# Six edge passes written without hardware loops, and 192 tiles' attention scalars gathered by GpSimd beside a shortened lookup loop

## The chip, the core and the metric

The kernel runs on one core of a Trainium2 chip. TensorE (PE) does matrix products into PSUM, VectorE (DVE) and ScalarE (ACT) do elementwise work, GpSimd (POOL) issues the indirect DMAs here, and SyncE (SP) issues the others. Each engine has its own instruction stream; they meet at semaphores. The metric is the device time of one execution in microseconds, the median over runs of the same kernel; lower is better. The profile is of one execution.

## What is computed

A graph with 6250 nodes of 128 features and 106,250 directed edges sorted by destination goes through four blocks, each followed by `x = layernorm(x + block(x))`:

```python
edge_index = jnp.stack([src, dst])
x = _layernorm(x + _L0_gnn_ref(...))   # mean of neighbours' rows, then a linear layer
x = _layernorm(x + _L1_gnn_ref(...))   # SAGE, SAGE, GAT (2 heads), RGCN (4 relations), fusion
x = _layernorm(x + _L2_gnn_ref(...))   # edge MLP with batch norm, summed by source
x = _layernorm(x + _L3_gnn_ref(...))   # 8 relations, edge weights
```

Every block contains a sum over edges, `segment_sum(table[src] * weight, dst)`. The attention layer also needs one pair of scalars for each edge, looked up by its source:

```python
al_src = (h * a_src).sum(-1)
al_dst = (h * a_dst).sum(-1)
e = jax.nn.leaky_relu(al_src[src] + al_dst[dst], 0.2)
```

## The kernel before

The edges lie in 832 tiles of 128 (T = 832, U = 16, ITERS = 52). `aggregate` sums over edges and is called six times, in this order: block0, sage1, sage2, gat, rgcn and block3. For each tile POOL gathers 128 rows of the table by an indirect DMA into one of U = 16 message buffers (line 387). DVE builds a one-hot matrix of the edges' positions in a window of 128 nodes (`one_hot`, lines 399 and 402; two for gat's two heads), PE multiplies the message by it into one of HU = 8 PSUM windows (line 534), and DVE adds the window into the accumulator at a node offset that depends on the data (line 458). DVE reads eight such offsets at a time into registers (`bases`, line 295), twice in 16 tiles. Four conditions tie the engines together: POOL reuses a message buffer when PE's product of 16 tiles earlier is done (`tile_done`); PE waits for the one-hot (`hot_ready`), for the gather to land (`gathered`) and, every second tile, for a window that DVE has added (`window_used`); DVE waits for `tile_done`.

POOL's stream in `aggregate` is already written out, one instruction a gather. PE, DVE, ACT (sage1's edge sort) and SP (gat's own rows) run hardware loops (`Fori`), whose body is one turn of 16 tiles; in block0's second part and in sage1 it is three and four turns. In a loop the semaphore values and the columns of the tables follow the loop's variable, so that register instructions stand before the waits and the operands. Line 487 is DVE's and line 552 PE's loop in gat and rgcn, 492 DVE's in block3. Five more jobs ride along in the turns: block0 counts and ranks the edges by source, sage1 sorts records, gat adds each node's own term, rgcn adds a part of the fusion (line 419), and block0 adds a bias.

`attention_terms` comes between sage2 and the softmax. POOL first writes 49 scatters of `al` to `t_last` (line 1414) and waits for them. Beside it the other engines look the source's two scalars up for all 832 tiles, four tiles (a quad) at a time: SP loads the keys (line 1408), PE spreads them over the partitions (line 1507), ACT makes a one-hot of them (lines 1368 and 1370), PE looks up with 12 matmuls (line 1498), DVE multiplies by a second one-hot and reduces (lines 1472, 1481, 1463), and ACT stores the result in `m.e` (line 1424). The first iteration of eight quads is written out, the other 25 are a loop. The next stage starts behind a barrier.

Of the kernel before, what the change touches and what calls it, by code (L numbers as in the profile page):

```python
# [26 lines left out]
P = 128  # L27
# [4 lines left out]
NT = -(-NODES // P)  # L32
# [3 lines left out]
ROWS = NT * P  # L36
# [3 lines left out]
QU = 4  # L40
QUADS = U // QU
ITERS = -(-EDGES // (P * U))
T = ITERS * U
EB = -(-T // P)
TP = EB * P
# [10 lines left out]
G = 13  # L56
# [260 lines left out]
def aggregate(nc, m, phase, table, index, weights, blocks, clear=True, degree=False, clears_tables=False, slots=False, sorts=None, own=False, fuses=None, loads=(), chunks=None, bias=None):  # L317
# [9 lines left out]
    n = e.passes  # L327
# [3 lines left out]
    with ExitStack() as ctx:  # L331
        sb, pb, sem = place(nc, ctx, phase)
# [25 lines left out]
        if own:  # L358
            @block.sync
            def _(sp):  # L360
                with sp.Fori(0, NT, 1) as it:
                    sp.wait_ge(own_made, it)
                    sp.dma_start(own_rows[:], table[bass.ds(it * P, P), :]).then_inc(own_in, 16)

# [5 lines left out]
        if sorts:  # L370
            @block.sync
            def _(sp):
                sort.load(sp)

            @block.scalar
            def _(act):
                with act.Fori(0, G, 1) as n:
                    for q in range(GT // QU):
                        sort.spread_low(act, n, q)

# [14 lines left out]
        def _(dve):  # L395
# [75 lines left out]
                    sort.keep(dve, of_sort[0])  # L471

            if slots:
                with dve.Fori(0, G, 1) as it:
                    turn(it, False, counts=it)
                order.find_starts(dve)
                dve.wait_ge(weights_in, 16 * len(loads))
                for first, last, added in ((0, NG, bias), (NG, G, None)):
                    with dve.Fori(first, last, 1) as n:
                        for r in range(TURNS - 1):  # L480
                            turn(n * (TURNS - 1) + (G + r), False, ranks=(n, r), bias=added if r == 0 else None)
            elif sorts:
                with dve.Fori(0, G, 1) as n:
                    for r in range(TURNS):
                        turn(n * TURNS + r, False, of_sort=(n, r))
            elif own or fuses:
                with dve.Fori(0, NT, 1) as it:
                    turn(it, True)
                with dve.Fori(NT, ITERS, 1) as it:
                    turn(it, False)  # L490
            else:
                with dve.Fori(0, ITERS, 1) as it:
                    turn(it, False)

        @block.tensor
        def _(pe):
            def own_terms(it):
                pe.wait_ge(own_in, 16 * (it + 1))
                pe.wait_ge(own_hot_ready, heads * (it + 1))
                pe.wait_ge(own_used, it)  # L500
                for b in range(blocks):
                    for j in range(heads):
                        f = (j * blocks + b) * P
                        last = nc.tensor.matmul(ps_own[:, b, :], own_rows[:, f:f + P], own_hot[:, j * P:(j + 1) * P],
                                                start=(j == 0), stop=(j == heads - 1))
                last.then_inc(own_made, 1)

            def fuse(it):
                pe.wait_ge(own_used, it)
                for k in range(2):  # L510
                    last = nc.tensor.matmul(ps_own[:, 0, :], fuses.weight[:, k, :], fuses.nodes[:, k, bass.ds(it * P, P)], start=(k == 0), stop=(k == 1))
                last.then_inc(own_made, 1)

            def turn(it, nodes_too, counts=None, ranks=None, of_sort=None):
                for u in range(U):
                    k = u % HU
                    if u % 2 == 0:
                        pe.wait_ge(e.window_used, used0 + it * U + u + 2 - HU)
                    if counts is not None and u % 2 == 1:
                        order.add_up(pe, counts, u // 2)  # L520
                    if ranks is not None:
                        order.rank_up(pe, ranks[0], ranks[1] * U + u)
                    if of_sort is not None:
                        sort.move(pe, of_sort[0], of_sort[1] * U + u)
                    if nodes_too and own and u == HU:
                        own_terms(it)
                    if nodes_too and fuses and u == HU:
                        fuse(it)
                    pe.wait_ge(e.hot_ready, hots0 + (it * U + u + 1) * heads)
                    pe.wait_ge(e.gathered[u], 16 * (turns0 + it + 1))  # L530
                    for b in range(blocks):
                        for j in range(heads):
                            f = (j * blocks + b) * P
                            last = nc.tensor.matmul(ps[k][:, b, :], message[u][:, f:f + P], hot[:, u, j * P:(j + 1) * P],  # L534
                                                    start=(j == 0), stop=(j == heads - 1))
                    if degree:
                        last = nc.tensor.matmul(ps[k][:, 1, :], m.ones[:], hot[:, u, :], start=True, stop=True)

                    last.then_inc(e.tile_done, 1)

            if slots:
                with pe.Fori(0, G, 1) as it:
                    turn(it, False, counts=it)
                with pe.Fori(0, G, 1) as n:
                    for r in range(TURNS - 1):
                        turn(n * (TURNS - 1) + (G + r), False, ranks=(n, r))
            elif sorts:
                with pe.Fori(0, G, 1) as n:
                    for r in range(TURNS):
                        turn(n * TURNS + r, False, of_sort=(n, r))  # L550
            elif own or fuses:
                with pe.Fori(0, NT, 1) as it:
                    turn(it, True)
                with pe.Fori(NT, ITERS, 1) as it:
                    turn(it, False)
            else:
                with pe.Fori(0, ITERS, 1) as it:
                    turn(it, False)


# [812 lines left out]
def attention_terms(nc, m, a):  # L1373
# [3 lines left out]


    AQ = 8
    AITERS = T // (AQ * QU)  # L1380
    assert T % (AQ * QU) == 0
    with ExitStack() as ctx:
        sb, pb, sem = place(nc, ctx, "al")
        table, rest, part = m.al, sb("rest", [P, 2, NT]), sb("part", [P, 2, NT])
# [2 lines left out]
        low_hot, distance = sb("low_hot", [P, 2, QU * P], BF16), sb("distance", [P, 2, QU * P])  # L1387
        high_hot, product = sb("high_hot", [P, 2, QU, NT]), sb("product", [P, 2, QU, 2, NT])
        picked = sb("picked", [P, 2, QU, 2])
        ps_low = [pb(f"ps_low{k}", [P, QU * P]) for k in range(2)]  # L1390
        ps = [pb(f"ps{k}", [P, QU, P]) for k in range(2)]
        keys_in, spread, low_ready, looked, high_ready, product_ready, reduced, kept = (
# [5 lines left out]

        @block.sync
        def _(sp):  # L1400
            sp.wait_ge(ints_padded, 2)
            for k, name in enumerate(("dst", "edge_type_4")):
                load_edges(sp, m.edge_ints[:, k], a[name], 1, ints_in)
            sp.wait_ge(ints_in, 96)
            with sp.Fori(0, AITERS, 1) as it:
                for q in range(AQ):
                    sp.wait_ge(spread[q], it)
                    sp.dma_start(keys[:, q], row_of(m.t_low_dst[bass.ds(((it * AQ + q) * QU) * P, QU * P)])).then_inc(keys_in[q], 16)

        @block.gpsimd  # L1410
        def _(pool):
            for j in range(NT):
                rows = P if j < NT - 1 else TAIL
                pool.indirect_dma_start(m.t_last, bass.IndirectOffsetOnAxis(ap=m.last_edge[0:rows, j:j + 1], axis=0), table[0:rows, j, :],
                                        None).then_inc(placed, 16)
            pool.wait_ge(placed, 16 * NT)

        @block.scalar
        def _(act):
            def keep(it, q):  # L1420
                act.wait_ge(zeroed, 1)
                act.wait_ge(reduced[q], it + 1)
                tiles = bass.ds((it * AQ + q) * QU, QU)
                nc.scalar.copy(m.e[:, :, tiles].rearrange("p k t -> p t k"), picked[:, q % 2]).then_inc(kept[q], 1)
# [15 lines left out]
                look(it, False)  # L1440
            for q in range(AQ - 2, AQ):
                keep(AITERS - 1, q)

        @block.vector
        def _(dve):
# [1323 lines left out]
def gnn_blocks(nc, a):  # L2769
    with ExitStack() as ctx:  # L2770
        sb, _, sem = place(nc, ctx, "all")
        m = Memory()
# [3 lines left out]
        table = lambda name, *shape: nc.dram_tensor(name, shape, F32, kind="Internal").ap()  # L2776
# [3 lines left out]
        m.t_hidden, m.t_self = table("t_hidden", C, T2 * P), table("t_self", TP * P, 2)  # L2780
        m.t_chunks, m.t_rec_dst = table("t_chunks", TABLE + G * P * CHUNKS, CHUNK * REC), table("t_rec_dst", P, TP * REC)
        m.t_rec = m.t_chunks[0:TABLE, :].rearrange("c (r k) -> (c r) k", k=REC)
        m.t_last = table("t_last", TP * P, 4)
        m.t_attr = nc.dram_tensor("t_attr", (ATTR, TP * P), BF16, kind="Internal").ap()
        m.t_w1c = nc.dram_tensor("t_w1c", (ATTR, C), BF16, kind="Internal").ap()
        m.t_low_dst, m.t_low = (nc.dram_tensor(n, (TP * P,), BF16, kind="Internal").ap() for n in ("t_low_dst", "t_low"))
# [98 lines left out]
```

## Time and profile before

| | |
|---|---|
| time, median of 3 runs | 10762.2 us (10758.03 to 10766.74) |
| the profiled execution's own time | 10761.99 us |
| its span, first to last instruction | 10760.2 us |
| instructions in the span | 143680 |
| busy share: PE, DVE, ACT, POOL | 57%, 47%, 14%, 59% |
| mean granted TensorE clock | 0.707 |
| HBM read and written | 794.65 MB, 144.18 MB |

An engine's busy time counts instructions that its datapath runs; register, branch and semaphore instructions belong to its sequencer and aren't in it. "Idle before" is the time in which an engine had no instruction before the ones of the row, with what ended most of it; "issue" means that the profile shows nothing that was waited for, and "remote" a semaphore event without a named instruction. Where a row says x832, 832 instructions are in the group. A table by window gives for each stretch its length and, for each engine, busy time and number of instructions.

### The profile page before, as it was taken

Reading aid. Unit: us, or ns where it says so; the run is one execution under the profiler, and the core shown is the slowest. Engines: PE = TensorE matmul, PEld = TensorE weight load, DVE = VectorE, ACT = ScalarE, POOL = GpSimd, SP = SyncE. Lnnn points to the kernel's source line nnn. Section 1 sums busy time; section 2 is a strip of 40 time slices with the busy share of each in tenths; the row PEclk is TensorE's granted clock in tenths of the full one; section 3 lists DMA queues with packets and bytes.
Section 4 is the critical chain, followed back from the end, with each engine's and each line's share of the span. In section 5 each row is a group of like instructions: output and inputs, shape, how many; then the busy total and the mean of one; then the engine's idle time right before and its main releaser. Section 6 shows DMA issues by size and latency. Waiting matters only on the chain. (4 is left out here: it accounts for less than half of the span.)

```text
span 10760.2 us, 143680 instructions
## 1 busy us (share of the span) xinstructions
PE 6118.1 (57%) x32219; PEld 5125.3 (48%) x32219; DVE 5059.5 (47%) x17185; ACT 1560.0 (14%) x3639; POOL 6324.8 (59%) x6901
## 2 busy tenths in 40 slices
PE   4555566665555546755777753444555567853333
PEld 4445455554555533535777633333444456733332
DVE  6666755554444421685666633334211115733334
ACT  0000033332000001740000000000221225710000
POOL 6666466775666662106666546664566666646665
PEclk7777778887666668558999965555666768965555
DMA  2111211112333312005666521112655656421111
GB/s 78 43 45 45 59 47 45 45 45 61 90 91 90 91 55 73 4 11 145 185 185 185 165 79 46 46 46 57 147 156 155 159 155 145 151 92 46 46 46 47
DMA packets 651433, 941.53 MB, mean 88 GB/s; under 512 B 253820, under 2 KB 427892, under 8 KB 650812
## 3 DMA queue, kind: packets, MB, share of 16 engines
q0 software_dynamic: 252288, 606.77, 21.1%
q1 hardware_dynamic: 299360, 328.15, 9.9%
q10 hardware_dynamic: 99548, 4.42, 0.8%
q14 instruction: 207, 1.70, 0.1%
q8 instruction: 30, 0.49, 0.0%
HBM read 794.65 MB, written 144.18 MB: 87 GB/s over the span
## 5 line engine op out<-in xcount | busy, mean ns | idle before, releaser
L534 PE MATMUL block_windows<-block_hot,block_message 128*128 128x128 f32 x3328 | 871.1, 393 | 881.3 <-DVE third_acc L458 418.1
L534 PE MATMUL sage_windows<-sage_hot,sage_message 128*128 128x128 f32 x4992 | 959.3, 357 | 584.2 <-DVE sage_hot L402 396.2
L534 PEld LDWEIGHTS sage_windows<-sage_hot,sage_message 128*128 128x128 f32 x4992 | 925.1, 267 | 679.3 <-DVE sage_hot L402 452.7
L534 PEld LDWEIGHTS block_windows<-block_hot,block_message 128*128 128x128 f32 x3328 | 741.0, 286 | 979.9 <-issue 624.2
L2214 POOL DMA_INDIRECT eh_message<-t_q,all_position x896 | 848.5, 947 | 533.3 <-issue 248.0
L387 POOL DMA_INDIRECT block_message<-t_rel,all_src x832 | 789.8, 949 | 576.2 <-issue 209.3
L387 POOL DMA_INDIRECT sage_message<-t_x,all_src x832 | 870.4, 1046 | 425.4 <-issue 217.2
L387 POOL DMA_INDIRECT rgcn_message<-t_rel,all_src x832 | 788.7, 948 | 520.9 <-issue 204.4
L458 DVE TENSOR_TENSOR first_acc<-first_acc,sage_windows 128x128 f32 (+1 forms) x1664 | 588.2, 353 | 1063.9 <-remote 596.6
L387 POOL DMA_INDIRECT block_message<-in_x,all_src x832 | 818.8, 984 | 434.7 <-issue 204.0
L534 PE MATMUL gat_windows<-gat_hot,gat_message 128*128 128x128 f32 x6656 | 901.9, 293 | 287.9 <-issue 207.6
L387 POOL DMA_INDIRECT gat_message<-t_h,all_src x832 | 790.0, 949 | 461.9 <-remote 202.9
L387 POOL DMA_INDIRECT sage_message<-t_s,all_src x832 | 789.5, 949 | 458.6 <-issue 197.7
L534 PEld LDWEIGHTS gat_windows<-gat_hot,gat_message 128*128 128x128 f32 x6656 | 852.7, 208 | 333.7 <-issue 331.6
L838 PE MATMUL sage_ps_sort<-first_acc,sage_sort_low_hot 128*128 128x272 f32 x1664 | 601.1, 495 | 444.6 <-DVE first_acc L803 183.5
L2244 DVE TENSOR_SCALAR_CACHE_REDUCE eh_hot<-eh_low_rows,all_column 128x128 f32<-128x128 bf16 x896 | 248.2, 343 | 1100.6 <-DMA eh_low_rows<-t_low 805.1
L534 PE MATMUL rgcn_windows<-rgcn_hot,rgcn_message 128*128 128x128 f32 x1664 | 441.5, 437 | 559.0 <-DVE second_acc_rgcn L458 311.0
L2271 PE MATMUL eh_ps<-eh_hot,eh_window 128*128 128x128 f32 x1792 | 517.9, 385 | 379.6 <-issue 246.7
L534 PEld LDWEIGHTS rgcn_windows<-rgcn_hot,rgcn_message 128*128 128x128 f32 x1664 | 376.5, 319 | 619.9 <-issue 425.3
L2271 PEld LDWEIGHTS eh_ps<-eh_hot,eh_window 128*128 128x128 f32 x1792 | 407.2, 280 | 463.8 <-issue 335.3
L838 PEld LDWEIGHTS sage_ps_sort<-first_acc,sage_sort_low_hot 128*128 128x128 f32 x1664 | 361.2, 241 | 528.0 <-issue 412.9
L458 DVE TENSOR_TENSOR second_acc<-second_acc,gat_windows 128x256 f32 x832 | 347.9, 418 | 406.9 <-remote 247.5
(474 smaller groups left out, 11739.8 us busy)
## 6 DMA issues: line engine op xcount, KB each, us to landing
eh_window<-t_p SPq DMA_DIRECT2D x896, 64.0 KB
t_hidden<-eh_hidden SPq DMA_DIRECT2D x112, 512.0 KB
sc_rows<-t_hidden SPq DMA_DIRECT2D x112, 512.0 KB
eh_low_rows<-t_low SPq DMA_DIRECT2D x112, 256.0 KB
t_rel<-n_h SPq DMA_DIRECT2D x49, 512.0 KB, 2.6
eh_message<-t_q,all_position POOLq DMA_INDIRECT x896
block_message<-in_x,all_src POOLq DMA_INDIRECT x832
sage_message<-t_x,all_src POOLq DMA_INDIRECT x832
```

What stands on the lines that cost most here:

```text
L387: pool.indirect_dma_start(message[u][:], None, table, bass.IndirectOffsetOnAxis(ap=index[:, it * U + u:it * U + u + 1], axis=0)).then_inc( ...
L458: nc.vector.tensor_tensor(window, window, ps[k], ALU.add).then_inc(e.window_used, 1)
L534: last = nc.tensor.matmul(ps[k][:, b, :], message[u][:, f:f + P], hot[:, u, j * P:(j + 1) * P], start=(j == 0), stop=(j == heads - 1))
L838: last = self.nc.tensor.matmul(self.ps[:, 0:SPAN * REC], self.low_hot[:, k, t], self.masked[:, k, t].rearrange("p h k -> p (h k)"), start= ...
L2214: pool.indirect_dma_start(message[:, u, :], None, m.t_q, bass.IndirectOffsetOnAxis(ap=m.dst[:, it * U + u:it * U + u + 1], axis=0)).then_i ...
L2244: nc.vector.tensor_scalar(hot[:, q, e], rows, m.column[:], 0.0, ALU.is_equal, ALU.add, accum_out=m.of_source[:, bass.ds(it * U + q * QU + ...
L2271: nc.tensor.matmul(ps[q][:, e], window[:, u, :], hot[:, q, e], start=False, stop=False, skip_group_check=True)
```

## The change

Every `Fori` in `aggregate` becomes a Python loop, so that all 52 turns of each pass are written out, with constants for the semaphore values and table columns. What the turns do and wait for stays; the node offsets are still read into registers. In `attention_terms` the lookup loop covers 20 iterations (640 tiles) in place of 26. SP writes `al` to a new table in memory, `t_al`. POOL, after its 49 scatters, waits for that table and gathers the pairs of the last 192 tiles from it, one indirect DMA a tile, into `rows_got`, with a wait in front of each batch of 16 for the batch two before it. At the end ACT waits for all of them and copies them into `m.e`.

```diff
-                with sp.Fori(0, NT, 1) as it:
+                for it in range(0, NT):
                     sp.wait_ge(own_made, it)
...
-                with act.Fori(0, G, 1) as n:
+                for n in range(0, G):
                     for q in range(GT // QU):
                         sort.spread_low(act, n, q)
...
             elif sorts:
-                with dve.Fori(0, G, 1) as n:
+                for n in range(0, G):
                     for r in range(TURNS):
                         turn(n * TURNS + r, False, of_sort=(n, r))
             elif own or fuses:
-                with dve.Fori(0, NT, 1) as it:
+                for it in range(0, NT):
                     turn(it, True)
-                with dve.Fori(NT, ITERS, 1) as it:
+                for it in range(NT, ITERS):
                     turn(it, False)
             else:
-                with dve.Fori(0, ITERS, 1) as it:
+                for it in range(0, ITERS):
                     turn(it, False)
...
-    AITERS = T // (AQ * QU)
-    assert T % (AQ * QU) == 0
+    AITERS = 20
+    LOOKED = AITERS * AQ * QU
+    GOT = T - LOOKED
+    assert 0 < GOT and GOT % 16 == 0
...
+        rows_got = sb("rows_got", [P, GOT, 4])
+        got = [sem(f"got{k}") for k in range(2)]
+        table_kept = sem("table_kept")
...
+            sp.dma_start(m.t_al.rearrange("(j p) w -> p j w", p=P), table[:]).then_inc(table_kept, 16)
             sp.wait_ge(ints_padded, 2)
...
+            pool.wait_ge(table_kept, 16)
+            for n in range(GOT):
+                batch, turn = divmod(n, 16)
+                if batch >= 2 and turn == 0:
+                    pool.wait_ge(got[batch % 2], 16 * 16 * (batch // 2))
+                pool.indirect_dma_start(rows_got[:, n, :], None, m.t_al,
+                                        bass.IndirectOffsetOnAxis(ap=m.src[:, LOOKED + n:LOOKED + n + 1], axis=0)).then_inc(got[batch % 2], 16)
             pool.wait_ge(placed, 16 * NT)
...
+            for k in range(2):
+                act.wait_ge(got[k], 16 * sum(1 for n in range(GOT) if n // 16 % 2 == k))
+            nc.scalar.copy(m.e[:, :, LOOKED:T].rearrange("p k t -> p t k"), rows_got[:, :, 0:2])
```

The same replacement stands in PE's three branches and in DVE's branch for block0, not shown.

## Rows read from the trace of the kernel before

**Rows 1.** Page: busy time by engine, and its slices of POOL, TensorE clock and DMA.

```profile
PE 6118.1 (57%) x32219; PEld 5125.3 (48%) x32219; DVE 5059.5 (47%) x17185; ACT 1560.0 (14%) x3639; POOL 6324.8 (59%) x6901
...
POOL 6666466775666662106666546664566666646665
PEclk7777778887666668558999965555666768965555
DMA  2111211112333312005666521112655656421111
```

**Rows 2.** Windows of the six passes and the lookup loop: length, then busy time (x instructions).

```profile
core 0: us, PE busy (x) PEld busy (x) DVE busy (x) ACT busy (x) POOL busy (x), PEclk, DMA share, GB/s
50.00:650.00 600.00, 321.59 (x1799) 294.42 (x1799) 386.44 (x1112) 0.00 (x0) 398.27 (x402) 0.73 0.18 47
1350.00:2540.00 1190.00, 765.52 (x3251) 631.94 (x3252) 683.78 (x2040) 400.79 (x1010) 843.50 (x808) 0.80 0.17 45
2700.00:3870.00 1170.00, 636.80 (x3226) 597.12 (x3227) 480.83 (x1615) 0.00 (x0) 764.95 (x807) 0.68 0.31 90
4910.00:6140.00 1230.00, 951.80 (x6912) 888.54 (x6913) 782.79 (x2594) 0.00 (x0) 778.63 (x821) 0.93 0.65 185
6270.00:7450.00 1180.00, 480.25 (x1826) 407.05 (x1827) 436.17 (x1674) 0.00 (x0) 777.71 (x822) 0.53 0.18 46
9510.00:10690.00 1180.00, 436.12 (x1639) 365.36 (x1638) 423.02 (x1625) 0.00 (x0) 781.50 (x825) 0.54 0.18 46
```

**Rows 3.** Timeline of rgcn from 7020.5 us: start, duration, instruction, [idle before].

```profile
7020.53 0.95 POOL L387 DMA_INDIRECT rgcn_message<-t_rel,all_src  x1 [0.30 <-issue]
7023.60 0.95 POOL L387 DMA_INDIRECT rgcn_message<-t_rel,all_src  x1 [2.12 <-remote]
```

**Rows 4.** Timeline of gat from 5510.8 us.

```profile
5510.87 0.27 PE L534 MATMUL gat_windows<-gat_hot,gat_message 128*128 128x128 f32 x1 [0.25 <-issue]
...
5511.60 0.36 PE L534 MATMUL gat_windows<-gat_hot,gat_message 128*128 128x128 f32 x1 [0.46 <-issue]
5512.31 0.27 PE L534 MATMUL gat_windows<-gat_hot,gat_message 128*128 128x128 f32 x1 [0.35 <-issue]
...
5513.02 4.28 PE L534 MATMUL gat_windows<-gat_hot,gat_message 128*128 128x128 f32 x36 [0.44 <-issue]
```

**Rows 5.** Timeline of the lookup's first 70 us, DVE's products, SP's keys, POOL's last scatter.

```profile
4309.55 67.61 SPq L1408 DMA_DIRECT2D al_keys<-t_low_dst  x18
...
4316.21 0.57 DVE L1481 TENSOR_TENSOR al_product<-al_ps,al_high_hot 128x392 f32<-128x392 f32 x1 [9.94 <-DMA neigh_neigh_bias<-in_L_gnn_b_neigh]
...
4337.23 0.57 DVE L1481 TENSOR_TENSOR al_product<-al_ps,al_high_hot 128x392 f32<-128x392 f32 x1 [19.72 <-remote]
...
4361.60 1.57 POOL L1414 DMA_INDIRECT t_last<-all_al,all_last_edge  x1 [0.30 <-issue]
4368.02 0.57 DVE L1481 TENSOR_TENSOR al_product<-al_ps,al_high_hot 128x392 f32<-128x392 f32 x1 [29.47 <-issue]
```

**Rows 6.** Windows: 45.7 us beside POOL's scatters, and 313 us without POOL.

```profile
4316.30:4362.00 45.70, 3.39 (x26) 2.09 (x26) 2.52 (x6) 3.00 (x6) 34.72 (x37) 0.50 0.03 2
4380.50:4693.50 313.00, 313.00 (x2505) 201.36 (x2502) 251.62 (x577) 289.16 (x578) 0.00 (x0) 0.50 0.00 1
```

**Rows 7.** Groups of 4380.5 to 4693.5 us, and POOL's small gathers of the softmax.

```profile
L1370 ACT ACTIVATE al_low_hot<-al_distance,all_ones 128x512 bf16<-128x512 f32 x193 | 139.3, 722 | 6.4
...
L1652 POOL DMA_INDIRECT softmax_rows<-t_self,all_last_edge x49 | 46.4, 947 | 487.3 <-SPq L1621 472.7 <-issue 14.6
```

**Rows 8.** Timeline at the end of the lookup: ACT's last store.

```profile
4702.88 0.20 ACT L1424 COPY attention_e<-al_picked 128x8 f32<-128x8 f32 x1 [1.26 <-DVE al_picked L1463]
```

**Rows 9.** DMA queues that load instructions: sage1 (first two rows), sage2 (last).

```profile
q14 instruction: 81, 0.66, 0.2%
q8 instruction: 2, 0.03, 0.0%
...
q14 instruction: 7, 0.06, 0.0%
```

More of the change, by code:

```diff
@@ L473, in _ @@
             if slots:
-                with dve.Fori(0, G, 1) as it:
+                for it in range(0, G):
                     turn(it, False, counts=it)
@@ L478, in _ @@
                 for first, last, added in ((0, NG, bias), (NG, G, None)):
-                    with dve.Fori(first, last, 1) as n:
+                    for n in range(first, last):
                         for r in range(TURNS - 1):
@@ L541, in _ @@
             if slots:
-                with pe.Fori(0, G, 1) as it:
+                for it in range(0, G):
                     turn(it, False, counts=it)
-                with pe.Fori(0, G, 1) as n:
+                for n in range(0, G):
                     for r in range(TURNS - 1):
@@ L547, in _ @@
             elif sorts:
-                with pe.Fori(0, G, 1) as n:
+                for n in range(0, G):
                     for r in range(TURNS):
@@ L551, in _ @@
             elif own or fuses:
-                with pe.Fori(0, NT, 1) as it:
+                for it in range(0, NT):
                     turn(it, True)
-                with pe.Fori(NT, ITERS, 1) as it:
+                for it in range(NT, ITERS):
                     turn(it, False)
             else:
-                with pe.Fori(0, ITERS, 1) as it:
+                for it in range(0, ITERS):
                     turn(it, False)
@@ L2782, in gnn_blocks @@
         m.t_rec = m.t_chunks[0:TABLE, :].rearrange("c (r k) -> (c r) k", k=REC)
-        m.t_last = table("t_last", TP * P, 4)
+        m.t_last, m.t_al = table("t_last", TP * P, 4), table("t_al", ROWS, 4)
         m.t_attr = nc.dram_tensor("t_attr", (ATTR, TP * P), BF16, kind="Internal").ap()
```

## The prediction, made before the changed kernel was built or run

> **What bounds the kernel now.** I read the page's busy shares and its 40 slices first, then the windows of the six passes, then single instructions inside them. No engine is full: POOL has the most, 59%, and in the passes' slices it stands at 6 or 7 tenths with DMA mostly at 1 or 2 [rows 1]. In the windows of the passes POOL works two thirds of the time, PE between 37% and 77%, DVE 34 to 64% [rows 2]. So the passes are bounded by a handover, not by a datapath.
>
> A gather occupies POOL 0.95 us and the next follows after 0.30 us of issue [rows 3]: 1.25 us each, 20.0 us for a turn of 16 tiles. The passes need more. From the gathers in each window [rows 2], 16 of them take 600/402 x 16 = 23.9 us in block0, 1190/808 x 16 = 23.6 in sage1, 23.2 in sage2, 24.0 in gat, 23.0 in rgcn and 22.9 in block3. What stands above 20.0 is POOL waiting for `tile_done`, as the 2.12 us in [rows 3]. Over 52 turns and six passes: (3.9 + 3.6 + 3.2 + 4.0 + 3.0 + 2.9) x 52 = about 1070 us, of which POOL waits some 955 (sage1's gathers are themselves a little longer, 843.50/808 = 1.04 us, and a few of the window's POOL instructions aren't gathers). 955 us is the ceiling of what the first part can bring.
>
> Why does POOL wait, when PE and DVE have time to spare? In gat PE starts one matmul each 0.7 us (5510.87, 5511.60, 5512.31), each only 0.27 to 0.36 us long, and then, in the stop of POOL, 36 of them back to back in 4.28 us [rows 4]. The same picture stands in the lookup. While POOL scatters, the quads of `attention_terms` come 21.0 and 30.8 us apart (4316.21, 4337.23, 4368.02); POOL's last scatter starts at 4361.60 and ends at 4363.17, and 4.9 us later the quads run [rows 5]. Then they take 313.0/(578/3) = 1.624 us each, with ACT busy 289 of 313 us (a quad is three instructions of ACT, x193 for each line) [rows 6, 7]. In 45.7 us beside the scatters PE did 26 matmuls where it does 366 without them [rows 6]. I read this as: while POOL issues indirect DMAs back to back, every other engine's stream advances in steps of 0.7 us, and catches up when POOL stops.
>
> **Part 1, the passes.** Removed are, per tile and estimated from the code, some 1.5 register or branch instructions of PE's stream and 2.5 of DVE's; 832 x 6 tiles make 7,500 and 12,500. All wait conditions, gathers, matmuls and DVE operations stay, and so does `bases`. None of it shortens POOL's 20.0 us for a turn; what can shrink is the stop. SP's and ACT's loops (gat's rows, sage1's sort) are off this path: ACT has 400 us of work in sage1's 1190, and gat's own rows are one load a turn.
>
> What a removed instruction is worth I take from passes that differ in work per tile. Matmuls and weight loads for a tile: gat 2 x 6912/821 = 16.84, sage2 2 x 3226/807 = 8.0, block3 2 x 1639/825 = 3.97 [rows 2]. From sage2 to gat a turn grows by 0.77 us, 0.087 for each instruction a tile; from block3 to sage2 by 0.32 us, 0.079. So the engines' work weighs little: twice as much makes the stop only a quarter longer. By 0.083 us a turn, PE's 1.5 give 0.083 x 1.5 x 52 x 6 = 39 us, PE's and DVE's 4 together 104 us if both lay on the path in turn. I take 70. The bounds are 0 (the steps belong to waits and datapath instructions, all of which stay) and 150 (a register instruction costs more than a matmul's step).
>
> The price of straight code is its supply. Sage1, whose turns stand four times in the loop's body, loads 83 packets of instructions and sage2 7 [rows 9], and the two differ by 0.36 us a turn, 19 us over the pass; at most 19/76 = 0.25 us a packet, all put down to them. Seven packets for sage2's written-out 807 gathers are some 115 instructions each. The six passes hold about 52,400 instructions of PE and DVE, estimated from the windows' counts and the code's waits, so some 456 packets: below 115 us, and near 0 if they are loaded ahead. I count nothing, since sage1's queue was busy 0.66 us in all [rows 9], and keep the bound as a rival.
>
> **Part 2, the lookup.** Now its loop ends with ACT's store at 4702.88 [rows 8]. Removed: six iterations, 48 quads x 1.624 = 78 us. Added on SP: one store of `al`, ahead of the loads of integers and keys in its queue; it is out some tens of us before POOL's 49 scatters end, and hides behind them. Added on POOL: 192 gathers. The nearest row is the softmax's small gathers, 947 ns with 14.6/48 = 0.30 us of issue [rows 7], so 192 x 1.25 = 239 us, with the waits on `got` met long before (the batch was issued 20 us earlier). POOL starts them where its scatters end, 4363.2, and ends at 4602.6. In terms of POOL this fits beside 112 quads with room to spare. But it puts POOL back into the state in which a quad takes 21 to 31 us [rows 5].
>
> Step by step: from 4316.2, the first quad's product, to 4602.6 are 286.4 us, in which 286.4/30.8 = 9.3 to 286.4/21.0 = 13.6 quads follow it; 10.3 to 14.6 of 160 are done. POOL stops, recovery takes 4.9 us as at 4368.02, and 145.4 to 149.7 quads follow at 1.624: 236 to 243 us. The loop ends at 4607.4 + 240 = 4847, to 4851 at most, 4844 at least. ACT's copy of 192 x 2 values adds 0.5 to 1 us (a store of 8 takes 0.20 [rows 8]), and the next stage stands behind a barrier, so all of it reaches the end. 4848.5 - 4702.9 = **+146 us**. The quads beside gathers may also go faster than beside scatters (0.95 against 1.57 us [rows 3, 5]). Gathers leave no more room between issues, 0.30 us in both [rows 3, 5], and gat's matmul each 0.7 us stood beside gathers. By those 0.7 us a quad, which has 13 matmuls and as many loads, would take about 26 x 0.7 = 18 us: 15.7 quads in 286 us, no different. The bounds are the two below: no slowing (-78) and no progress at all, 4607.4 + 159 x 1.624 = 4866, +164.
>
> **Sum.** The profiled execution: 10762.0, its span 10760.2 and 1.8 around it; the median is 10762.2. 10762 + 146 - 70 = **10838 us**. With part 1 between 0 and 150: 10908 to 10758.
>
> **Rivals.** *Loops are what holds the engines in the passes* (faster). If a large part of the 0.7 us steps are branches and register instructions, or what follows a branch, the stops shrink far more than by the slope. A third of them, 318 us: 10762 + 146 - 318 = 10590. For it: each turn of the loops ends in a branch, and gat's single matmuls are shorter than their spacing [rows 4], so something else fills the time. Against: the 0.7 us steps stand inside a turn as well, and sage1, with one branch in four turns, is not faster than sage2 with one in each [rows 2]. It decides from a gain above 150 us. The Trainium skill, "Runtime: NRT & Kernel Launch", section on instruction fetch, says that a taken branch breaks the sequential prefetch and that kernels prefer full unrolling where possible; by that rule straight code is the faster one, and this rival is what it would make here. The packets show only that loops load less [rows 9].
>
> *The lookup runs at full speed beside the gathers* (faster). Then its loop goes on from 4368.0 with 158 quads: 4624.6, 78 us earlier, and 10762 - 78 - 70 = 10614. It needs the 21 and 31 us to come from something else than POOL, as SP's keys, 18 loads spread over 67.61 us [rows 5]. Against: the release comes within 5 us of POOL's last scatter, and 26 matmuls in 45.7 us [rows 6] isn't a matter of keys alone. Between this and the forecast lies a loop that is slowed partly; it breaks even on part 2 where 48 quads fit into the gathers' 239 us.
>
> *Straight code isn't supplied in time* (slower still). If each packet stalls its engine by 0.23 us in a pass, that is 456 x 0.23 = 105 us where the forecast has none, and nothing is gained: 10762 + 146 + 105 = 11013. The point is a stall that isn't caught up in POOL's burst, since POOL runs 4 to 16 gathers ahead. Against: POOL's own written-out stream shows 0.30 us between gathers throughout [rows 3].
>
> **How the numbers follow.** Forecast 0.55, loops 0.23, full speed 0.12, supply 0.10. About 0.2%, 21 us, is what a measurement of this kernel can tell from no change. Of the forecast's 0.55, 0.07 lie within 21 us of the time before (part 1 at 125 to 150) or next to it; the two faster rivals have 0.35, of which 0.01 falls short. Faster 0.34, same 0.08, slower 0.58. The range reaches from below the first two rivals, 10560, to above the forecast's own upper end, 10930; outside stay the supply rival and the deep end of the first. The forecast's own range is 10758 to 10908.
>
> **What the profile after would show.** Part 2: 192 gathers of POOL 1.25 us apart from 4363 to 4603, `al_product` every 21 to 31 us until then, the stage ending about 4848; at 4625 the third case holds, and any rate above one quad in 5 us makes the part a gain. Part 1: paces lower by 0.2 us a turn in all six passes, POOL's stops still some 3 us long a turn; stops of 2 us or less mean the first rival. The instruction queues show some 450 packets more; a pass slower than before means they cost. I would be wrong above all if POOL's gathers from a small table leave the others more room than its scatters do, or if what moves in 0.7 us steps is the register instructions themselves.

## The result, and the profile after

The changed kernel takes 10859.9 us (median of 4 runs, 10850.7 to 10862.7) where the kernel before takes 10763.7: a ratio of 1.0088, with a 95% interval of 1.0071 to 1.0106. That is 96 us slower. The forecast was 10838. The profiled execution has a span of 10848.9 us, 88.7 more than before.

First the page of the changed kernel: busy time, and the two queues that load instructions.

```profile
PE 5979.3 (55%) x31595; PEld 4980.0 (46%) x31595; DVE 5020.3 (46%) x17041; ACT 1494.9 (14%) x3496; POOL 6519.6 (60%) x7093
...
q8 instruction: 205, 3.36, 0.1%
q14 instruction: 281, 2.30, 0.1%
```

No engine has changed its share by more than two points [rows 1]; POOL has 192 instructions more. The six passes, each in a window of its own (length, then busy time and instructions by engine, as in [rows 2]):

```profile
core 0: us, PE busy (x) PEld busy (x) DVE busy (x) ACT busy (x) POOL busy (x), PEclk, DMA share, GB/s
50.00:650.00 600.00, 318.68 (x1823) 290.55 (x1822) 390.47 (x1130) 0.00 (x0) 409.14 (x409) 0.72 0.18 48
1330.00:2500.00 1170.00, 710.54 (x3232) 589.67 (x3232) 689.41 (x2023) 399.75 (x1004) 840.15 (x806) 0.81 0.17 46
2650.00:3810.00 1160.00, 629.30 (x3237) 582.48 (x3235) 504.87 (x1606) 0.00 (x0) 764.07 (x806) 0.68 0.32 92
5040.00:6240.00 1200.00, 951.60 (x6825) 892.12 (x6826) 770.73 (x2565) 0.00 (x0) 779.07 (x811) 0.91 0.66 189
6390.00:7550.00 1160.00, 464.51 (x1818) 376.69 (x1819) 429.62 (x1665) 0.00 (x0) 770.83 (x813) 0.57 0.18 46
9620.00:10770.00 1150.00, 454.55 (x1603) 353.14 (x1603) 414.79 (x1593) 0.00 (x0) 764.30 (x808) 0.54 0.18 46
```

Length by gathers times 16 gives 23.5, 23.2, 23.0, 23.7, 22.8 and 22.8 us a turn, against 23.9, 23.6, 23.2, 24.0, 23.0 and 22.9 before [rows 2]. From the start of its first to that of its last gather each pass is 14.2, 16.6, 10.6, 15.2, 10.7 and 9.7 us shorter, **77 us** in sum.

The lookup goes the other way. DVE's products beside POOL's gathers, POOL's last gather, TensorE's next matmuls, and the end of the stage:

```profile
4528.93 0.57 DVE L1497 TENSOR_TENSOR al_product<-al_ps,al_high_hot 128x392 f32<-128x392 f32 x1 [35.09 <-issue]
...
4560.66 1.09 POOL L1427 DMA_INDIRECT al_rows_got<-t_al,all_src  x1 [0.30 <-issue]
4565.33 0.57 DVE L1497 TENSOR_TENSOR al_product<-al_ps,al_high_hot 128x392 f32<-128x392 f32 x1 [35.09 <-issue]
...
4570.97 1.16 PE L1514 MATMUL al_ps<-al_parts,al_low_hot 128*128 128x98 bf16 x12 [34.70 <-ACT al_low_hot L1370]
...
4589.14 0.57 DVE L1497 TENSOR_TENSOR al_product<-al_ps,al_high_hot 128x392 f32<-128x392 f32 x1 [22.50 <-issue]
...
4833.87 0.20 ACT L1437 COPY attention_e<-al_picked 128x8 f32<-128x8 f32 x1 [1.26 <-DVE al_picked L1479]
4833.98 0.85 ACT L1458 COPY attention_e<-al_rows_got 128x384 f32<-128x384 f32 x1
```

A quad comes each 36.4 us (4528.93, 4565.33), seven times in a row. The ninth product starts 3.6 us after the last gather's end (4561.75), the tenth at 4589.14, and then the loop runs at 1.63 us a quad. From POOL's first scatter to the softmax's first copy the stage takes 583.5 us against 404.3: **+179 us**. 179 less 77 are 102; the 88.7 of the spans come with another 13.5 us that stages with unchanged code are shorter by (the edge MLP 6.5 of them).

### The profile page after: what moved, and what is told of

It reads as the page before. It is cut to its first block and busy times, and to the rows that moved or that the text cites. A ratio compares the mean times of both kernels' runs of the same rounds, so it can differ in the third digit from the quotient of the medians.

```text
span 10848.9 us, 122823 instructions
## 1 busy us (share of the span) xinstructions
PE 5979.3 (55%) x31595; PEld 4980.0 (46%) x31595; DVE 5020.3 (46%) x17041; ACT 1494.9 (14%) x3496; POOL 6519.6 (60%) x7093
## 5 line engine op out<-in xcount | busy, mean ns | idle before, releaser
L534 PE MATMUL block_windows<-block_hot,block_message 128*128 128x128 f32 x3328 | 893.5, 391 | 832.5 <-DVE third_acc L458 416.5
L534 PE MATMUL sage_windows<-sage_hot,sage_message 128*128 128x128 f32 x4992 | 935.0, 349 | 586.2 <-DVE first_acc L458 356.3
L534 PEld LDWEIGHTS sage_windows<-sage_hot,sage_message 128*128 128x128 f32 x4992 | 888.9, 258 | 684.3 <-DVE first_acc L458 388.5
L534 PE MATMUL gat_windows<-gat_hot,gat_message 128*128 128x128 f32 x6656 | 939.3, 297 | 317.9 <-issue 224.6
L534 PEld LDWEIGHTS gat_windows<-gat_hot,gat_message 128*128 128x128 f32 x6656 | 876.1, 210 | 376.5 <-issue 363.3
L838 PE MATMUL sage_ps_sort<-first_acc,sage_sort_low_hot 128*128 128x272 f32 x1664 | 563.8, 470 | 472.5 <-DVE first_acc L803 308.0
L534 PEld LDWEIGHTS rgcn_windows<-rgcn_hot,rgcn_message 128*128 128x128 f32 x1664 | 349.7, 292 | 714.3 <-DVE second_acc_rgcn L458 352.6
L458 DVE TENSOR_TENSOR third_acc<-third_acc,block_windows 128x128 f32 x832 | 239.4, 288 | 713.5 <-remote 447.8
```

The costliest lines, as they stand in the source:

```text
L458: nc.vector.tensor_tensor(window, window, ps[k], ALU.add).then_inc(e.window_used, 1)
L838: last = self.nc.tensor.matmul(self.ps[:, 0:SPAN * REC], self.low_hot[:, k, t], self.masked[:, k, t].rearrange("p h k -> p (h k)"), start= ...
```

## The experiments

The chips fall into two kinds. The traces of before and after show stops and slow quads. The experiments ran on chip 11, where the kernel before takes 10865 us and every trace shows the same stops, and on chips 5 and 4, where it takes 9339 and 9355 us and the traces show none to speak of. I call the first kind held and the second free. Each kernel was timed against the kernel before on its own chip. Of the kernel before and of the changed one there are traces from the first measurement alone, whose chip isn't on record. It was held but not like chip 11: with the same code the six passes take 7206 us in the changed kernel's trace and 7284 us in that of e1b on chip 11, a difference as large as what the passes gain. So e1b's gain is read from its timing beside the kernel before, not from the traces. Chip 11 was held at two times, chips 5 and 4 were free at one time each; whether it is the chip, or something else that was there at the time, no run separates.

From POOL's first scatter to the softmax's first copy, all kernels:

| kernel | held chips | free chip 5 |
|---|---|---|
| before, or passes alone (e1, e1b) | 404.3, 404.6 us | 353.5 us |
| the change, or its lookup alone (e2) | 583.5 us | 315.5 us |
| gathers after the loop (e3, e3b) | 581.7 us | 536.3 us |
| 1.2 gathers a quad (e4, e4b) | 411.7 us | 314.8 us |
| a third of the lookup's matmuls (e5) | 532.7 us | |
| memsets for gathers (e6) | 326.4 us | |

**Each part alone (chip 5, free).** e1 has the changed `aggregate` and the old lookup, e2 the old `aggregate` and the changed lookup.

> Part 1 alone: the six passes written out, the lookup as before. In the trace of the changed kernel the six passes' gathers (first to last) are 77 us shorter in sum (14.3, 16.5, 10.6, 15.2, 10.7, 9.8) and the other stages some 14 us. If the two parts don't touch each other: 10764 - 77 to 91 = 10673 to 10687. If part of what the passes gained comes from the changed lookup or its place in the code, less: above 10700.

> Part 2 alone: loops kept, 192 gathers beside a lookup loop of 20 iterations. The changed kernel's lookup, from POOL's first scatter to the last store, took 582 us where it took 402.7: +179. So 10764 + 179 = 10943, if the parts add up. If instead the written-out passes make the lookup slower (its loop's instructions stand behind far more code), less than +160.

Measured: e1 9343.8 against 9339.2, ratio 1.0005 (0.9996 to 1.0014); e2 9298.9, ratio 0.9954 (0.9939 to 0.9969). Neither expectation holds: they were worked out for a held chip, and this one is free. Windows of e1: gat and rgcn.

```profile
4270.00:5280.00 1010.00, 880.80 (x6900) 810.84 (x6899) 780.78 (x2591) 0.00 (x0) 764.78 (x806) 1.00 0.76 223
5420.00:6420.00 1000.00, 632.09 (x1794) 436.86 (x1794) 469.58 (x1652) 0.00 (x0) 756.03 (x801) 0.50 0.20 53
```

Here 16 gathers take 1010/806 x 16 = 20.0 us, POOL's floor of [rows 3], with 0.95 us busy and 0.30 of issue. POOL never stops, so there is nothing that written-out code could shorten, and no cost of its supply shows either. And e2 beside its gathers, 220 us:

```profile
3776.00:3996.00 220.00, 219.56 (x1763) 141.42 (x1761) 177.13 (x407) 202.52 (x405) 165.72 (x174) 0.50 0.06 2
```

405 ACT instructions, three a quad, are 135 quads in 220 us: 1.63 us each beside 174 gathers. On this chip the change does what it says.

**The passes alone (chip 11, held).** The kernel of e1 again.

> The same kernel as e1_passes_only, six passes written out and the lookup as before, wanted on a chip with the slowdown. There the kernel after 49 scatters and memsets took 10705 beside 10877 before, of which the lookup explains 78 (48 quads), so some 94 are left for the passes. Theory, written-out code shortens the stops of POOL: 75 to 95 us less than before, ratio 0.991 to 0.993. Rival, the 94 are the difference between single executions: ratio 0.997 to 1.003. On a chip without the slowdown: 1.0005 again.

Measured: 10783.3 against 10865.0, ratio 0.9929 (0.9911 to 0.9946), 82 us less, as expected. It agrees with the 77 us of the two traces, and separates the part from the lookup.

**Gathers after the loop.**

```diff
             pool.wait_ge(table_kept, 16)
+            pool.wait_ge(kept[AQ - 1], AITERS)
```

> The changed kernel with POOL's 192 gathers held back until the last quad is stored, so nothing runs beside them. Theory: beside back-to-back gathers the others as good as stand still (36.4 us a quad in place of 1.62), so overlapping them is worth nothing: the loop ends at 4253 + 63 + 5 + 158 x 1.624 = 4577, the gathers add 192 x 1.25 to 1.28 = 240 to 246, end 4818 to 4825 against 4834 with overlap; 10845 to 10852, a little faster than the changed kernel. Rival, the overlap hides a useful part and the loss lies elsewhere (a table write, the end of the stage): more than 10900.

> The same kernel as e3_after_loop, wanted on a chip with the slowdown: gathers only after the last quad. 26 TensorE instructions a quad at 1.40 us each beside gathers (36.4 with 26, 14.0 with 10) mean that some 7 quads, 11 us, run beside the 240 us, and their release came 28 us after the last gather's start; so serial is 0 to 20 us faster than the changed kernel, the stage from the first scatter to the last store 560 to 582 us against 582. Rival, overlap is worth something on this chip: over 600. On a chip without the slowdown 9528 again.

Measured: on chip 5 9528.3, ratio 1.0197 (1.0181 to 1.0213), so there the overlap is worth 221 us of the stage (536.3 against e2's 315.5). On chip 11 one execution took 10969.9 (before: 10865.0), 105 us more, where the changed kernel took 96 more in the first measurement. Its stage takes 581.7 us, against 583.5 with overlap in the changed kernel: the overlap is worth nothing there. The last quad and POOL's first and last gather in e3b:

```profile
4625.35 0.20 ACT L1438 COPY attention_e<-al_picked 128x8 f32<-128x8 f32 x1 [1.26 <-DVE al_picked L1480]
4626.34 0.99 POOL L1428 DMA_INDIRECT al_rows_got<-t_al,all_src  x1 [262.09 <-ACT attention_e L1438]
...
4866.78 0.95 POOL L1428 DMA_INDIRECT al_rows_got<-t_al,all_src  x1 [0.30 <-issue]
```

**One gather at a time.**

```diff
             for n in range(GOT):
+                quad = n * (LOOKED // QU) // GOT
+                pool.wait_ge(kept[quad % AQ], quad // AQ + 1)
```

> The changed kernel with POOL waiting, before gather n, for the quad 160 n / 192 to be stored: 1.2 gathers a quad, spread over the loop. Theory a, a gather takes its 1.25 us from everybody wherever it stands: 158 x 1.624 + 240 us as in the serial kernel, 10845 to 10870. Theory b, what stops the others is that POOL has the next gather queued behind each: with pauses a gather's 0.95 us hide beside a quad and the stage ends near 4577 + 10 to 40 us: 10605 to 10640. Theory c, a single gather delays a quad by more than its own length: the stage gets longer than with all of them back to back, above 10900.

> The same kernel as e4_one_a_quad, wanted on a chip with the slowdown: each gather waits for its quad, 1.2 gathers a quad. If only an unbroken row of gathers holds TensorE, and each pause of POOL lets it catch up, a quad takes 1.63 to 3 us and the stage from the first scatter to the last store 320 to 550 us. If TensorE gets one instruction for each 1.40 us whenever a gather is under way and runs freely otherwise, a quad takes 1.63 + 1.2 x 1.25 = 3.1 us, 560 us in all, as serial. If a single gather costs more than its length, over 600.

> The kernel of e4 once more, timed on a chip with the slowdown, as the candidate that beats both: passes written out, 1.2 gathers for each quad. Its single execution there was 10795 where the kernel before took 10865: ratio 0.992 to 0.995 against before; with the lookup taking 412 us against 583 in the changed kernel, some 170 us under that one. On a chip without the slowdown 0.995, as e4.

Measured on chip 11: one execution of 10794.9 (before: 10865.0), the stage 411.7 us. Theory a (560 us) and theory c fall. Theory b has the right sign but not the size: by its 4577 + 10 to 40 the stage would have been 334 to 364 us. A window of e4b, 327 us beside its gathers:

```profile
4375.00:4702.00 327.00, 257.12 (x2026) 162.95 (x2026) 201.22 (x467) 234.70 (x467) 177.96 (x187) 0.50 0.05 2
```

Two of its gathers in the timeline, with what they waited for:

```profile
4387.94 0.94 POOL L1429 DMA_INDIRECT al_rows_got<-t_al,all_src  x1 [2.84 <-ACT attention_e L1439]
...
4391.20 0.94 POOL L1429 DMA_INDIRECT al_rows_got<-t_al,all_src  x1 [0.89 <-ACT attention_e L1439]
```

467 ACT instructions are 156 quads in 327 us: 2.10 us each with 187 gathers among them, where 36.4 us stood beside an unbroken row in the changed kernel. On the free chips the pauses cost nothing: 0.9952 (0.9937 to 0.9967) on chip 5, as e2 without them, and 0.9967 (0.9953 to 0.9981) on chip 4. e4c ran on chip 4 too, so on a held chip this kernel has one execution and no interval.

**Fewer TensorE instructions (chip 11).** The kernel computes with one of the table's three bf16 parts, so its attention terms are less exact.

```diff
-                    for n in range(3):
+                    for n in range(1):
...
-parts[:, n].rearrange("p k j -> p (k j)"), start=(n == 0), stop=(n == 2))
+parts[:, n].rearrange("p k j -> p (k j)"), start=(n == 0), stop=(n == 0))
```

> The changed kernel with 4 matmuls for a quad's lookup in place of 12 (only the first of the three bf16 parts of the table, so the attention terms are less exact): TensorE has 5 matmuls and 5 loads a quad in place of 13 and 13. Where a quad beside POOL's gathers takes 36.4 us (the profiled chip): if each TensorE instruction is held 0.7 us, the 16 fewer save 11 to 22 us a quad (it comes to 14 to 25 us); if it is the waits between engines that are held, it stays at 34 to 37 us. Where a quad takes 1.63 us beside the gathers (the chip of the first four experiments), it stays 1.63, since ScalarE is what bounds it.

Measured: 10902.1 (one execution; before 10876.9). A window of the changed kernel, 212 us beside gathers:

```profile
4346.00:4558.00 212.00, 10.17 (x78) 6.28 (x78) 7.84 (x18) 9.01 (x18) 159.53 (x166) 0.50 0.06 2
```

A window of e5, 235 us beside gathers:

```profile
4365.00:4600.00 235.00, 17.81 (x85) 6.70 (x85) 22.32 (x51) 25.09 (x51) 177.88 (x183) 0.50 0.06 2
```

Three of e5's products in the timeline:

```profile
4444.25 0.56 DVE L1497 TENSOR_TENSOR al_product<-al_ps,al_high_hot 128x392 f32<-128x392 f32 x1 [13.05 <-issue]
...
4457.93 0.57 DVE L1497 TENSOR_TENSOR al_product<-al_ps,al_high_hot 128x392 f32<-128x392 f32 x1 [12.37 <-issue]
...
4471.93 0.57 DVE L1497 TENSOR_TENSOR al_product<-al_ps,al_high_hot 128x392 f32<-128x392 f32 x1 [12.69 <-issue]
```

TensorE does 78 matmuls in 212 us, 2.72 us each, and 85 in 235, 2.76 us each. The number of other instructions and waits of a quad is the same, yet a quad takes 14.0 us in place of 36.4. Divided by TensorE's loads and matmuls: 36.40/26 = 1.40 and 14.0/10 = 1.40 us. So beside this long row a quad's length goes with the number of its TensorE instructions, 1.40 us for each, twice the 0.7 us that the expectation had. It isn't the waits between engines. The 36.4 us are from the first measurement and not from chip 11; that chip 11 holds about as much is seen beside the scatters, where two products of e4b stand 32.9 us apart (4330.91, 4363.84). In e5 the release came 25.8 us after the last gather's end (4610.43 to 4636.27), so that time doesn't go with the length of the quad under way.

**POOL busy without DMAs (chip 11).**

```diff
-                pool.indirect_dma_start(rows_got[:, n, :], None, m.t_al, ...)
+                nc.gpsimd.memset(rows_got[:], 0.0).then_inc(filled, 1)
+                pool.wait_ge(filled, n + 1)
```

> The changed kernel with 192 memsets of 128x768 on POOL, one after another, in the place of the 192 gathers (the last 192 tiles get no attention scalars). POOL is as busy, but writes no descriptors and starts no DMAs. On a chip with the slowdown: if it comes from indirect DMAs, quads run at 1.63 us right behind the 49 scatters and the stage ends near 4577; if it comes from a busy POOL, they stay at 20 to 36 us. On a chip without it: 1.63 us throughout.

Measured: 10705.1 (one execution; before 10876.9), the stage 326.4 us, near the expected 324 (4577 - 4253). e6's second and third products, beside the scatters and right behind them:

```profile
4352.44 0.57 DVE L1494 TENSOR_TENSOR al_product<-al_ps,al_high_hot 128x392 f32<-128x392 f32 x1 [24.01 <-remote]
...
4367.23 0.57 DVE L1494 TENSOR_TENSOR al_product<-al_ps,al_high_hot 128x392 f32<-128x392 f32 x1 [13.48 <-issue]
```

A window of e6, 144 us beside memsets:

```profile
4371.00:4515.00 144.00, 144.00 (x1152) 92.36 (x1149) 116.35 (x266) 133.12 (x267) 133.54 (x182) 0.50 0.00 1
```

POOL is busy 133.5 of 144 us, more than with gathers, and 89 quads run in it: 1.62 us each. The indirect DMAs hold the others, not a busy POOL. Which part of them does, POOL's own work for a transfer or the transfer, this run doesn't separate.

**Which stream matters in the passes.** e7 has only PE's loops written out, e8 only DVE's, both with the old lookup.

> Only TensorE's loops of the six passes written out, the rest and the lookup as before. Both engines' (with SP's and ScalarE's two) gave 82 us on a chip with the slowdown (10865 to 10783). The prediction's working put 39 us on TensorE's register instructions at 0.083 us each a turn: 10826, ratio 0.996 to 0.997. If TensorE alone is what POOL waits for (it is held 1.40 us an instruction beside gathers), nearly all: 0.993. If VectorE is the one, 0.999 to 1.001. On a chip without the slowdown 1.000.

> Only VectorE's loops of the six passes written out. The prediction's working, PE's 39 us of about 100 and a discount to 70: 31 to 65 us here, ratio 0.994 to 0.997. If TensorE alone is waited for: 0.999 to 1.001. If the two lie on the path in turn, this and TensorE's share add up to 0.993. On a chip without the slowdown 1.000.

Both ran on chip 4, which is free: 0.9997 (0.9987 to 1.0006) and 1.0008 (0.9998 to 1.0017). They say again that there is nothing to gain there; how the 82 us of a held chip divide between the two engines stays open, and with it the expectations for a held chip. Their instruction queues tell whose code the packets are: 205 on q8 and 207 on q14 for e7, 30 and 273 for e8, 30 and 207 before. They also size the change: e7 has 7,787 instructions fewer than before, e8 9,658.

## Why the prediction was right, step by step

**What bounds the kernel.** For the lookup the reading of [rows 5, 6], that the other engines crawl while POOL issues indirect DMAs back to back, is shown by e6 (not a busy POOL), e3b (the overlap is worth nothing) and e4b (pauses bring it back). For the passes I misread [rows 4]. The 36 matmuls in 4.28 us from 5513.02 don't stand in a stop of POOL. POOL's gathers around them, in the trace of before:

```profile
5511.08 0.94 POOL L387 DMA_INDIRECT gat_message<-t_h,all_src  x1 [0.30 <-issue]
...
5513.38 0.95 POOL L387 DMA_INDIRECT gat_message<-t_h,all_src  x1 [1.35 <-remote]
...
5514.63 0.95 POOL L387 DMA_INDIRECT gat_message<-t_h,all_src  x1 [0.30 <-issue]
...
5515.88 0.95 POOL L387 DMA_INDIRECT gat_message<-t_h,all_src  x1 [0.30 <-issue]
...
5517.14 0.95 POOL L387 DMA_INDIRECT gat_message<-t_h,all_src  x1 [0.30 <-issue]
```

The burst runs beside four gathers back to back, and the steps of 0.7 us stand beside the last gather of a row (5511.08) and in the stop behind it (5512.31, 5513.02). Counted over the whole pass, TensorE starts a matmul each 0.16 us beside unbroken gathers and each 0.34 us in POOL's stops, the reverse of what I wrote. So a short row doesn't hold TensorE from its start, and a stop doesn't let it catch up at once. Held and free chips do differ in these stops: e1b has them and e1 has none. What makes TensorE slow at the end of a row stays open. The forecast for the passes came from the slope between passes, not from this picture, and for that reason didn't suffer.

What I didn't see either is that the hold differs between the chips. e1 and e1b are one kernel on two chips, 9339.8 and 10773.8 us: of the 1434 us between them the six passes hold 870, the edge MLP 269, and the wait of POOL's first scatter behind the stage before it 183. On a free chip the rival "full speed beside the gathers" is the truth, and by e1 (no change) and e2 (40 us less) the change would have been some 40 us faster there, an estimate. The profile of a single chip can't tell: that the forecast comes near rests on the result coming from a held one.

**Part 1**, forecast -70, measured -77 from the traces and -82 timed. PE's count was near (7,787 removed, 7,500 forecast), DVE's too high (9,658 for 12,500); e1 has 18,862 fewer in all (143680 to 124818), the rest being ACT's and SP's. With these counts, 3.5 a tile, the slope of 0.083 us gives 90 us if both engines lie on the path in turn, against 77 to 82 measured. The slope was about right; that 70 came so near is in part luck, since the step from 104 down to 70 was a choice between 39 and 104 and not worked out. The split over the two engines wasn't tested on a held chip. The paces fell by 0.41, 0.33, 0.17, 0.30, 0.14 and 0.11 us a turn, more in block0, sage1 and gat, which have more riding on the turns.

**Part 2**, forecast +146, measured +179. Three terms were too small, all counted from POOL's first scatter. The gathers ended at 309.0 us, I had 302.4, since some were longer (1.09 us at 4560.66). The release came 27.4 us after the end of the last gather (4561.75 to 4589.14), I had 4.9 from [rows 5]: 22.5 us more. And 9 quads were done by then, not the 10.3 to 14.6 of the 21 to 31 us that scatters allow [rows 5], about 3.4 quads or 5.6 us more. Together 34.7, against 33 missing. The wrong step is to have carried the quad's pace and the recovery over from 49 scatters to 192 gathers. The 18 us a quad that I worked out from the 0.7 us steps was half of what it is (36.4), and even that came by counting twice: a step of 0.7 us in [rows 4] moves one matmul with its load, so that 13 steps would be 9 us. An instruction takes 1.40 us beside this row, not 0.35.

The store of `al` did not hide either: SP's first keys went out 21.0 us after the first scatter (4273.79 - 4252.77), against 9.3 before, and the first product stood at 28.3 instead of 16.0 us. On a held chip 12 us are a third of a quad of 36.4, so little of it reaches the end there. On chip 5 it is paid (26.1 against 13.9 us), and with POOL ending last it explains why e2 gained 38 us in the stage and not the 78 of the rival: 78 less 12, less 28 us from the last product to the softmax (4027.2 - 3996.4 = 30.8, before 2.9).

**The rivals.** "Loops are what holds the engines" falls: the turns still took 22.8 to 23.7 us where POOL's floor is 20.0, and the gain was 77 to 82 us, not 318. The Trainium skill's preference for full unrolling ("Runtime: NRT & Kernel Launch", the section on instruction fetch) is borne out in its sign on the held chip 11, 0.7%, and not at all on a free one, where 1.0005 was measured. Whether the 0.7% come from branches or from fewer instructions no run separates. "Straight code isn't supplied in time" falls on both: the queues loaded 486 packets and not 237 (249 more; I had estimated 456), and no pass was slower. **The sum** was 22 us short of the median and 12.7 short of the profiled execution (10850.7), and it was that near by luck in part, because errors met: 33 us too little for the lookup, against 7 too little gained in the passes and 13.5 in stages that the change doesn't touch. Why those are shorter isn't shown.

## A version for both kinds of chip

e4, with the passes written out and a gather for each stored quad, is the one I would keep. It takes 10795 (one execution) against 10865 on the held chip, where the changed kernel's lookup stage is 172 us longer than e4b's, and 0.9952 and 0.9967 of before on the free ones, as fast as the lookup's change alone. On a held chip the passes alone do as well (10783, e1b), since 411.7 us for e4b's lookup stage are no less than the 404.6 us of the old one.

## What to carry to other kernels

Ask of each overlap with GpSimd's indirect DMAs what the other engines did beside such a row in this chip's own trace, and lay GpSimd's lines beside the others' before saying which stood still; if they crawled, the row is serial time, and a wait of GpSimd on the others' progress after each transfer, which looks like a loss, gives it back. Price a stage beside a long unbroken row by the number of TensorE instructions in it. Short rows are another case: gat has 269 of them in a turn of 24 us, 0.09 us each. And before a profile is believed for all chips, take one of the same kernel on a second chip: here the two differ by 15%, fifteen times the effect of the change, and the change of the lookup has the opposite sign.

## What the runs showed of the hardware

- Two kinds of chips: with the same lookup code TensorE's loads and matmuls beside 192 back-to-back gathers take 1.40 us each on one (36.4 us a quad), and run at full rate on the other (135 quads in 220 us).
- Beside the first gathers of a short row TensorE runs at its full rate on a held chip too (36 matmuls in 4.28 us beside four gathers); the steps of 0.7 us stand at the row's end and behind it.
- Beside POOL's memsets, busy 93% of the time, nothing is held (e6).
- After the last of 192 gathers the others were held another 27.4 us (25.8 in e5), after 49 scatters 4.9 us; with pauses between gathers a quad takes 2.10 us. In the records TensorE's twelve matmuls of a quad start within 1.16 us (4570.97), and the product that waits for them starts 18 us later (4589.14). With e5's count beside it I read this as a hold between a matmul's recorded start and its signal. What on the chip causes it no run tells.
